# Slot rows without the residual, and a last scatter that adds into the output

## The reference

```python
x = x + attn(cond(x, ...))            # x: 8 x 256 tokens of 128; two layers of norm, k/v/r, scan, Wo
x = x + ffn(cond2(x, itok, ...), ...)

# cond2: y = x @ weight[category] + bias[category]
# ffn, top-1 gate over 8 experts, capacity 320 slots an expert:
gates = softmax(tokens @ wg); expert = argmax(gates)
pos   = rank of the token among those of its expert; keep = pos < 320
h     = relu(dispatched @ w1[e] + b1[e])            # 128 -> 512
out   = gate * (h @ w2[e] + b2[e])                  # 512 -> 128, zero for a token that isn't kept
```

## Time and profile before

| | us |
|---|---|
| median of 3 runs | 138.19 |
| lowest, highest | 137.83, 138.86 |
| span of the profiled execution | 137.7 |
| PE busy | 114.3 |
| DVE, ACT, POOL busy | 77.1, 61.0, 67.5 |

### The profile page before, as it was taken

How to read it: one execution, slowest core, us unless ns; L and a number is a source line. 1 busy time by engine, 2 the same in 40 slices (tenths; PEclk the granted TensorE clock), 3 DMA queues, 4 the chain that set the end, 5 groups by cost and what they waited for, 6 DMA issues and landing times.

```text
span 137.7 us, 1892 instructions
## 1 busy us (share of the span) xinstructions
PE 114.3 (83%) x567; PEld 80.2 (58%) x567; DVE 77.1 (56%) x255; ACT 61.0 (44%) x116; POOL 67.5 (49%) x88
## 2 busy tenths in 40 slices
PE   5951599999889899999999996299999999999100
PEld 2411254664737558879776442199888898689000
DVE  2899506799797976867455940045336436435100
ACT  3537648666466639463255800135423444322000
POOL 6457560009596688055277883000040762777730
PEclk9996558999999999999999999959999999999955
DMA  1999999970000003033252322699000000101100
GB/s 62 243 323 318 213 262 395 409 281 8 24 2 19 19 30 87 19 117 120 76 172 96 120 74 79 151 307 295 15 19 24 34 31 17 35 22 50 47 29 0
DMA packets 14409, 15.99 MB, mean 116 GB/s; under 512 B 1847, under 2 KB 11704, under 8 KB 14400
## 3 DMA queue, kind: packets, MB, share of 16 engines
q1 hardware_dynamic: 12736, 12.21, 30.5%
q0 software_dynamic: 1664, 3.68, 7.8%
HBM read 9.04 MB, written 7.11 MB: 117 GB/s over the span
## 4 chain that ended last, share of the span: by engine, by line
PE 62%; DVE 10%; issue 9%; POOL 8%; DMA 5%; ACT 2%; DVEq 0%; POOLq 0%
PE bank L573 11%; PE bank L740 11%; POOL slots L356 4%; PE bank L551 4%; PE bank L541 4%; PE bank L731 4%; PE bank L728 4%; PE bank L557 4%; PE bank L563 4%; PE bank L729 4%; PE bank L592 3%; PE bank L613 3%; POOL out L366 2%; DMA got<-slots 2%; DMA slots<-rows,slot 2%
## 5 line engine op out<-in xcount | busy, mean ns | idle before, releaser
L366 POOL DMA_INDIRECT out<-room,got x20 | 19.7, 983 | 28.4 <-DVE room L1089 24.5
L356 POOL DMA_INDIRECT slots<-rows,slot x16 | 16.8, 1052 | 12.0 <-DVE slot L978 7.8
L620 PE MATMUL bank<-warm,onesb 128*128 128x512 bf16 x77 | 18.8, 403 | 1.5 <-POOL warm L281 1.5
L307 POOL TENSOR_TENSOR rstd<-veps,mhalf 128x4 f32<-128x4 f32 x8 | 8.8, 1097 | 20.8 <-DVE veps L850 20.7
L740 PE MATMUL bank<-room,w_sb 128*128 128x320 f32 (+1 forms) x64 | 17.4, 413 | 0.1
L1073 DVE TENSOR_SCALAR room<-bank,par 128x320 f32<-128x320 f32 x16 | 8.8, 550 | 14.6 <-PE bank L731 14.6
L573 PEld LDWEIGHTS bank<-wt,y 128*128 128x128 f32 x64 | 15.5, 327 | 1.8 <-DVE y L879 1.8
L573 PE MATMUL bank<-wt,y 128*128 128x128 f32 x64 | 16.5, 401 | 0.0
L620 PEld LDWEIGHTS bank<-warm,onesb 128*128 128x128 bf16 x77 | 7.8, 103 | 11.1 <-issue 2.1
L740 PEld LDWEIGHTS bank<-room,w_sb 128*128 128x128 f32 x64 | 11.2, 190 | 3.6 <-DVE room L1073 0.2
L728 PE MATMUL bank<-gh,w1h 128*128 128x320 f32 x32 | 12.4, 388 | 0.4 <-ACT gh L496 0.4
(11 more groups left out here) (115 smaller groups left out, 200.9 us busy)
## 6 DMA issues: line engine op xcount, KB each, us to landing
w_sb<-w SPq DMA_DIRECT2D x8, 512.0 KB, 12.7
slots<-empty SPq DMA_DIRECT2D x4, 645.0 KB, 10.9
got<-slots SPq DMA_DIRECT2D x4, 325.0 KB, 5.4
room<-x SPq DMA_DIRECT2D x4, 256.0 KB, 4.4
out<-rows SPq DMA_DIRECT2D x4, 256.0 KB, 2.8
got<-slots SPq DMA_DIRECT2D x3, 320.0 KB, 5.6
wt<-wqkv SPq DMA_DIRECT2D x2, 256.0 KB, 4.7
out<-room,got POOLq DMA_INDIRECT x20, 2.2
```

The lines of the kernel that those rows point to most:

```text
L356: pool.indirect_dma_start(slots, bass.IndirectOffsetOnAxis(ap=slot[:, q, j:j + 1], axis=0), rows[:, q, j, :], None).then_inc(scattered, 16)
L366: pool.indirect_dma_start(out, bass.IndirectOffsetOnAxis(ap=got[:, i, c, TOK:TOK + 1].bitcast(I32), axis=0), fin[:, i, c, :], None, bounds ...
L620: pe.matmul(psK[:, :], onesb[:, :], warm[:, :], start=True, stop=True)
```

## The change

A slot row becomes 130 numbers: y, gate and token number. The residual x1 gets a tile of its own, `x1r`, from which PE transposes it and SP stores it to the output. The fills of empty rows, the scatter to the slots and the second read of each pair shrink with the row; their numbers stay. `finish` and `res_b2` no longer add x1: they are `tensor_scalar` (times the gate) instead of `scalar_tensor_tensor` (times the gate, plus x1). The last scatters get `compute_op=ALU.add`: the DMA adds its rows to those that stand in the output. On every engine the instructions stay the same in number and order.

```diff
-ROW = 2 * D + 2
-GATE, TOK = 2 * D, 2 * D + 1
+ROW = D + 2
+GATE, TOK = D, D + 1
...
+        x1r = sb("x1r", [128, Q, J, D])
...
-                sp.dma_start(out_q[q], rows[:, q, :, D:2 * D]).then_inc(out_first, 16)
+                sp.dma_start(out_q[q], x1r[:, q, :, :]).then_inc(out_first, 16)
...
                     pool.indirect_dma_start(
                         out, bass.IndirectOffsetOnAxis(ap=got[:, i, c, TOK:TOK + 1].bitcast(I32), axis=0),
-                        fin[:, i, c, :], None, bounds_check=NTOK - 1, oob_is_err=False).then_inc(out_done, 16)
+                        fin[:, i, c, :], None, bounds_check=NTOK - 1, oob_is_err=False,
+                        compute_op=ALU.add).then_inc(out_done, 16)
...
-                    last = pe.transpose(psX[:, j * 128:(j + 1) * 128], rows[:, q, j, D:2 * D], identf[:, :])
+                    last = pe.transpose(psX[:, j * 128:(j + 1) * 128], x1r[:, q, j, :], identf[:, :])
...
-                    dve.tensor_tensor(rows[:, q, :, D:2 * D], ps, xh[:, q, :, :], ALU.add).then_inc(res_ok, 1)
+                    dve.tensor_tensor(x1r[:, q, :, :], ps, xh[:, q, :, :], ALU.add).then_inc(res_ok, 1)
...
-                    dve.scalar_tensor_tensor(fin[:, i, c, :], bank[6 + e % 2][:, n * 128:(n + 1) * 128],
-                                             got[:, i, c, GATE:GATE + 1], got[:, i, c, D:2 * D], ALU.mult, ALU.add
-                                             ).then_inc(fin_ok, 1)
+                    dve.tensor_scalar(fin[:, i, c, :], bank[6 + e % 2][:, n * 128:(n + 1) * 128],
+                                      got[:, i, c, GATE:GATE + 1], None, ALU.mult).then_inc(fin_ok, 1)
...
-                dve.scalar_tensor_tensor(res_b2[:, c - 3, :], b2row[:, :], got[:, PAIRS - 1, c, GATE:GATE + 1],
-                                         got[:, PAIRS - 1, c, D:2 * D], ALU.mult, ALU.add).then_inc(res_b2_ok, 1)
+                dve.tensor_scalar(res_b2[:, c - 3, :], b2row[:, :], got[:, PAIRS - 1, c, GATE:GATE + 1],
+                                  None, ALU.mult).then_inc(res_b2_ok, 1)
```

## The result

| | before, us | changed, us |
|---|---|---|
| median (4 runs each) | 138.01 | 146.21 |
| lowest, highest | 136.98, 138.86 | 144.82, 146.74 |
| span of the profiled execution | 137.7 | 145.0 |

The ratio is 1.0576, with a 95% interval of 1.0496 to 1.0656: 8.0 us slower. Forecast were 141.1 us and a range up to 145.0. The direction was right; the size was not.

What follows compares the result with a forecast made beforehand. POOL's full queue of 13 output scatter issues was taken to set the end; -0.24 (slots landing) + 2.6 (longer issues) + 0.5 (last landing) = +2.9, so 138.19 + 2.9 = 141.1 us, range 137.8 to 145.0.

Steps and rivals of the forecast that it cites:

- POOL's full queue: Output scatters at the end, from 115.92 us: 13 issues without longer waits, so an issue's change moves the end 13 times.
- x: Lengthening of each output scatter's issue on POOL by adding: taken as 0.20 us, bounds 0 and 0.49, 13 times: +2.6.
- Case C: Adding has its own, much slower issue path on POOL: issue doubled, x = 0.98, about 153.5 us; chance 0.12.
- The room: POOL's 2.81 us of idleness before the full queue: lets the five issues ahead lengthen up to x = 0.50.
- y: Later landing of the last output scatter because of adding: +0.5 us, an estimate, bounds 0 and 2.59.
- The shorter landing in the slots: Turn from dispatch to experts: narrower rows let the last scatter to the slots land sooner, -0.24 us, bounds 0 and -0.24.
- The second reads in 8-byte pieces: Reads of the slots on SP's queue, only `finish` needs them: pair 1 comes no later, 0 us.
- DVE's products: 18 products of 342 ns become `tensor_scalar`: 14 ns less each, covered by POOL's queue except the first, so 0.
- D: Before the experts: shorter landing keeps PE's clock up, with x and y near 0; faster, 136.5 us; chance 0.12.
- The one on issue: Issue on POOL: many descriptors can be made before their number shows; by that x near 0, time 138.5 us.
- rival A: An adding scatter's issue on POOL costs what it did, x up to 0.08: 138.5 us, no change; chance 0.36.
- The one on the queue's rate: DMA queues at the end: adding gives two read descriptors per chunk and halves the rate; charged nothing at share 0.11.

Runs made afterwards that it cites:

- e7: Kernel before, with only the first 7 of the 20 output scatters adding: 138.77 us against 138.21, ratio 1.0051.
- e8: Kernel before, with only the last 13 of the 20 output scatters adding: 146.60 us, ratio 1.0629.
- e4: Changed kernel with output scatters of other shapes: pair 0 adds 32 to 128 rows, pair 1 half-width rows, pairs 2 and 3 the same without adding; no time given.
- e9: Changed kernel without the adding (narrow rows, last scatters overwrite), run again: 137.92 us against 138.02, ratio 1.0007.
- e2: Kernel before with the adding alone in the last scatters, slot rows still wide: 147.45 us, ratio 1.0322.
- e11: Kernel before with transposes back and DVE's products moved ahead, plus SP waiting for the last x load before the fills: 137.23 us, ratio 0.9925.
- e12: Kernel before with only SP's wait for the last x load ahead of the fills, run again: 137.19 us against 138.48, ratio 0.9899.
- e3: Kernel before with only SP's wait for the last x load ahead of the fills: 142.43 us, ratio 0.9975.
- e1: Changed kernel without the adding (narrow rows, last scatters overwrite): 142.94 us against 142.97, ratio 1.0001.
- the first set: The runs e1 to e4, beside which the kernel before took 142.97 us.

## Why the prediction failed in size, point by point

**POOL's full queue, right.** The bound was read correctly from the earlier trace rows: 13 issues without a gap, 2.5 us of room before them. e7 and e8 show both halves of it, and that the step of an issue counts once for each.

**x, the longer issue, mis-sized: this is the step that failed.** Taken was 0.20, with 0.49 as the upper bound; 13 times 0.20 made 2.6 of the forecast 2.9. Measured: 0.573. The bound came from counting accesses, three for two, and taking the whole issue as proportional to them. e4 shows that an issue is nearly all fixed (0.87 of 0.98 at 32 rows) and that adding has a surcharge that is mostly fixed too (0.46 at 32 rows). No row of the kernel before held such an issue, so the bound was a model and not a bound. Case C, a path of its own for adding, was nearer in its mechanism, a price that comes with adding whatever the rows, and in the queue of 18 that follows; its price of 0.98 was too high. The stretching of the scatters to the slots to 1501 ns was read as a hint that work in an issue grows with what it writes; e4 has a growth with rows of 2.3 ns for an adding and 1.1 for a plain one, which is 0.3 and 0.15 us in 128 rows.

**The room, right but its end is overrun.** The prediction said that the room holds up to x = 0.50. At 0.573 the five issues before the eighth need 2.87, 0.36 more than there was, and the queue grows backward to 18. 13 x 0.573 + 0.36 = 7.8. With y = 0.5 and nothing for the rows that makes 8.3; the two measured ratios are 8.0 and 8.5 us.

**y, right, by a guess.** No row of the kernel before showed such a landing, and the bounds were 0 and 2.59. Predicted +0.5; from the end of the last issue to the end of the span it is 0.5 more. (From issue to landing it is 1.1 more, of which 0.57 is the issue itself.)

**The shorter landing in the slots, too small to matter.** Predicted -0.24, seen -0.14 and more in the profiles (-0.15 in the first pair), in the time 0 within some half a microsecond (e9).

**The second reads in 8-byte pieces, right.** Pair 1 was not late: the first reads of pairs 1 to 3 land in 4.2 to 4.5 us where they took up to 5.9. The 8-byte pieces cost less than the wide ones, not nothing. These lines are from the view of source line 275 of the changed kernel:

```profile
L275 SPq DMA_DIRECT2D got<-slots x3: 526/527/969, 85.2 to 88.1; - x3
...
DMA to landing us min/median/max: 4.2/4.3/4.5
```

**DVE's products, right.** 342 ns before and after; the 14 ns expected from the simpler form did not come either.

**D, PE's clock, did not come; the clock took more than before.** PE stood idle for 3.34 us ahead of the transposes (3.44 before), and in the changed kernel the clock is at its low level there too (window of 90 to 91 us; columns as in the earlier trace rows):

```profile
90.00:91.00 1.00, 1.00 (x5) 1.00 (x5) 0.55 (x1) 0.19 (x1) 0.00 (x0) 0.50 0.96 166
```

The experts started 1.93 us earlier than before (86.46 for 88.39), but from the transposes of the first pair to those of the next PE took 7.48 us where it had taken 6.54. That is 0.94 lost at the low clock, and 1.0 reaches POOL's third issue. The prediction read this stretch from one execution. It differs between executions of one kernel: 6.54 and 7.37 in the two profiles of the kernel before, 7.48 and 6.49 in those of the changed one. That the mechanism of D exists shows in e2, where PE was idle for only 1.00 us ahead of the transposes: the clock stayed at its high level, and the same stretch took 5.14 us (from 87.97). e2's rows from 88 to 92 us:

```profile
88.00:90.00 2.00, 1.63 (x9) 1.09 (x10) 0.89 (x2) 0.77 (x2) 0.00 (x0) 1.00 0.94 251
90.00:92.00 2.00, 2.00 (x15) 1.92 (x14) 1.08 (x2) 1.06 (x3) 0.00 (x0) 1.00 1.20 310
```

**The two rules.** The one on issue ("DMA: Bandwidth & Descriptors", "Anatomy of one DMA — SWDGE (gpsimd) path", of the Trainium skill: many descriptors before their number shows) holds for plain scatters here: 32 or 128 rows are 0.87 or 0.98. It says nothing of adding, and rival A, which leaned on it, was wrong. The one on the queue's rate ("Collectives: The Full Stack", "Why ReduceScatter is half of AllGather", of the Trainium skill, said there of a step of a collective) was rightly charged nothing: POOL's queue had 2.6 times the packets, and the DMA share from 116 to 132 us rose from 0.11 to 0.28, far from full.

## What to carry to other kernels

When a queue engine issues without a gap at the end of a kernel, multiply every doubt about one issue by the length of the queue before anything else, and say what the queue would be if its room is used up. An operation that appears nowhere in the trace has no upper bound from a model of its parts; the range should then reach to a price of the order of the operation itself. An adding scatter isn't free bytes: here it cost 0.57 us more to issue than an overwriting one, so carrying 512 bytes more in each row was much the cheaper way. And before two single profiles are compared, look at PE's granted clock behind its longest idle stretch: here it moved one kernel's experts by 0.8 to 1.0 us from one execution to the next.

## What the runs showed of the hardware that was not expected

- An adding indirect DMA took 1.555 us of POOL for 128 rows and 1.33 for 32, where a plain one took 0.98 and 0.87; row width (256 or 512 bytes) made no difference.
- It brought the DMA engines 112 packets more per issue of 128 rows, in five kernels (changed, e2, e4, e7, e8). One packet for each row, where a plain issue puts its rows into 16, fits every count.
- Holding back the fills, which stand behind the x loads on the same queue, until these had landed took 0.8 to 1.0 us off the kernel in e11 and 1.3 to 1.4 in e12, and nothing that could be told in e3. By which path is in part open (e12).
- In the ten profiles with 3.3 to 3.8 us of idleness of PE ahead of the experts its granted clock fell to 0.50, and the stretch to the next pair's transposes took 6.0 to 7.5 us. In e4, after 2.04 us, it fell too, and the stretch took 6.58. In the three with 0.7 to 1.4 us (e1, e2, e3) the clock stayed at 1.00 and the stretch took 5.1 to 5.2.
- In the first set DVE (e1 and e3, 2.5 and 1.6 us near 124 us) and ACT (all four profiles) stood idle with no releaser that the profile knows, and the kernel before took 5 us more beside them. The record gives the same chip number for e12, where the kernel before took 138.48, so it is no lasting trait of that chip. The cause is open; nothing was tried on it.
